# A graph network kernel: the check of its input in pieces behind the first additions of the last pass, and the last edge tile as a group of its own

## The chip, the cores and the metric

The kernel runs on one core of one Trainium2 chip. The metric is the device time of one execution in microseconds (us). In the profile PE is TensorE, DVE is VectorE, ACT is ScalarE, POOL is GpSimd and SP is the engine that queues most DMAs.

## The reference

The graph has 3125 nodes with 128 features and 53125 edges, sorted by `dst`. Three SAGE convolutions are followed by one GINE convolution, each block behind a LayerNorm and a ReLU:

```python
h = jnp.maximum(_layernorm(x, axis=-1), 0.0)
x = x + L0(h)          # 3 x: (segment_sum(h[src], dst) / count) @ Wl.T + b + h @ Wr.T
h = jnp.maximum(_layernorm(x, axis=-1), 0.0)
messages = gelu(h[src] + edge_attr @ We1 ...) @ We2 ...   # _mlp(x[src] + edge_attr, We1, be1, We2, be2)
x = x + mlp(h + segment_sum(messages, dst), Wu1, bu1, Wu2, bu2)
```

## The kernel before

`fast_path` works in two stages, and five instruction streams (one for each engine) meet at semaphores.

**Stage one: the dense stage.** A matrix of edge counts (`f_adj`, one byte for each pair of nodes) is built from the edge list in 213 groups, `GB` in the code. A class `Plan` gives each step a slot; each engine walks the slots in order. From slot 213 on no edges are left, and PE runs the products of the count matrix with the three parts of h (`dense_unit`, L1132). The nodes are cut into 7 chunks c: six of 500 nodes, and chunk 6 with 125. For layer 0 and chunk 6 the chain is `dense_unit` (PE), `mean_rows` (DVE, L664, the sums times the inverse counts), `mix_layer` (PE, L1104 and L1107, which waits for `mean_rows`). On DVE `mean_rows(6)` comes in slot 222, behind `split_rest` (L635) and `split_low` (L640) of slot 221. On PE `mix_layer(6)` comes in slot 223, behind 9 dense units of the next layer's first chunk. A PE instruction that waits holds everything behind it.

**Stage two: the edge pass.** 416 tiles of 128 edges (`FT`) go in groups of 4 (`FTG`): 104 groups g before. Every ninth group up to 98 is "picked" (11 groups): its rows of h are taken from on-chip memory by matmuls with one-hot matrices (`take_sources`, L1183). The other 93 groups get theirs by indirect DMAs, one for each tile, which POOL issues (L545): 372 in a row. POOL writes into a ring of `RW = 6` groups, so the first tile of group number r (counted without the picked ones) waits until group r - 6 has been added. For each group:

- PE: `mix`, edge features times `We1`, two groups ahead (L1168)
- DVE: the one-hots of the destination nodes, two groups ahead (L751), the addition of the gathered rows, `pre` (L870), and one-hots for the picked groups (L771)
- ACT: GELU, `msg` (L997)
- PE: the sum over edges, message times one-hot (L1237)

Behind the last group of a chunk of nodes follow that chunk's node steps, at fixed distances in groups: `TAKE` 1 (ACT copies the sums, L982), `MIX` 2 (PE, L1197 and L1199), `SUM` and `UP` 3 (DVE L783, PE L1205, ACT L985), `DOWN` 4 (PE, L1209), `ADD` 5 (DVE, L787), `STORE` 9. Chunk 5 ends with group 100, chunk 6 with the last group.

**The check.** The fast path holds only for inputs with certain bounds on `dst`. `check_input` on DVE tests them (L802 to L835), PE turns the result into one number (L1218), and `keep_flag` writes it to `spill`. If it is set, a general path computes everything again. All of the check stands ahead of the loop over the groups, and PE waits for it ahead of group 0. The check also reads `order`, whose DMAs are queued behind the broadcast of `rstd`.

Of the kernel before, what the change touches and what calls it, by code (L numbers as in the profile page):

```python
# [17 lines left out]
P = 128  # L18
# [10 lines left out]
class Shapes:  # L29


    def __init__(self, n_nodes, n_edges):
# [20 lines left out]
        self.FG = -(-self.FT // self.FTG)  # L53
        self.SLOPE = P * self.FTG * n_nodes / n_edges
        self.window = [(max(0, int(g * self.SLOPE) - self.MARGIN - 1),
# [3 lines left out]
        self.picked = list(range(self.PERIOD - 1, self.FG - self.FTG, self.PERIOD))  # L59
# [14 lines left out]

    def tiles(self, g):
        return min(self.FTG, self.FT - g * self.FTG)
# [144 lines left out]
def fast_path(nc, s, t, table, counts, inv, outT, spill):  # L221
# [5 lines left out]
    EVEN = NP + NP % 2  # L227
    KEYS = s.A_COLS + s.DW * NB - s.B_FROM
# [9 lines left out]
    END = G + STORE + 1  # L238
    with ExitStack() as ctx:
# [104 lines left out]
        order_in, checked, flagged, be2_ready = sem("order_in"), sem("checked"), sem("flagged"), sem("be2_ready")  # L344

# [57 lines left out]
        def edge_columns(g):  # L403
            return t["edge_attr_T"][:, g * T * P:(g * T + s.tiles(g)) * P]
# [15 lines left out]
        def src_columns(i):  # L420
            g = s.picked[i]
            return t["src_row"][g * T * P:(g + 1) * T * P].partition_broadcast(P)
# [84 lines left out]
        def _(pool):  # L507
# [30 lines left out]
            for g in range(G):  # L538
# [3 lines left out]
                for j in range(s.tiles(g)):  # L542
                    if j == 0 and r >= RW:
# [3 lines left out]
                        in_offset=bass.IndirectOffsetOnAxis(ap=table_idx[:, g * T + j:g * T + j + 1], axis=0),  # L547
# [3 lines left out]
        def _(dve):  # L551
# [149 lines left out]

            dve.wait_ge(idx_in, 16)
            edge_keys(0, HEAD)
            dve.wait_ge(made, 3)
            for slot in range(plan.slots):
# [26 lines left out]
                for c in plan.due("rows_add", slot):  # L732
                    keep_rows(c)

# [11 lines left out]
            def window_onehots(g):  # L746
# [3 lines left out]
                for j in range(s.tiles(g)):  # L750
                    ins = dve.tensor_scalar(onehot[:, g % OH, j, 0:hi - lo], iota[:, 0:hi - lo], float(lo),  # L751
                                            dst_abs[:, g * T + j:g * T + j + 1], ALU.add, ALU.is_equal)
# [37 lines left out]
            def check_input():  # L790

                F, L = first[0:1, :], last[0:1, :]
                F2, L2, FB, LB = F[:, 0:NT:2], L[:, 0:NT:2], F[:, 1:NT:2], L[:, 1:NT:2]
                DG = s.DG
                n_at = [0]

                def more(count):
                    n_at[0] += count
                    return viol[0:1, n_at[0] - count:n_at[0]]

                def over(a, gap, b):
                    dve.scalar_tensor_tensor(out=more(a.shape[-1]), in0=a, scalar=float(gap), in1=b, op0=ALU.subtract,  # L802
                                             op1=ALU.is_gt).then_inc(checked, 1)
                over(L2, s.A_COLS // NB - 1, F2)
                over(F2[:, 0:DG], -float(s.B_FROM // NB), FB)
                over(LB, s.DW - 1, F2[:, 0:DG])
                over(L2[:, 0:DG], -1.0, F2[:, 1:DG + 1])
                over(F2[:, 1:DG + 1], s.DW, F2[:, 0:DG])
                over(F, -1.0, L)
                dve.tensor_scalar(bound[0:1, 0, :], iota[0:1, 0:G], s.SLOPE, -float(s.MARGIN), ALU.mult,  # L810
                                  ALU.add).then_inc(flagged, 1)
# [4 lines left out]
                over(bound[0:1, 0, :], 0.0, group_ends[0:1, 0, :])  # L816
                over(group_ends[0:1, 1, :], 0.0, bound[0:1, 1, :])
                small = [(0, 0.0, ALU.is_gt), (NT - 1, float(N - s.DW), ALU.is_lt)]
                small += [(s.DT * (g + 1), float(e), ALU.is_lt) for e, g in zip(s.node_end, s.build_group) if g + 1 < GB]
                for i, limit, op in small:  # L820
                    dve.tensor_scalar(more(1), F[:, i:i + 1], limit, None, op).then_inc(checked, 1)
                dve.wait_ge(checked, 8 + len(small))
                dve.memset(flag[:, :], 0.0).then_inc(flagged, 1)
                dve.wait_ge(flagged, 3)
                dve.tensor_reduce(flag[0:1, 0:1], viol[0:1, 0:n_at[0]], AX.X, ALU.max).then_inc(flagged, 1)
                dve.wait_ge(order_in, 32)
# [1001 lines left out]
```

## Time and profile before

| what | value |
|---|---|
| median of 3 runs | 976.62 us |
| lowest, highest of the 3 | 975.94, 2135.52 us |
| the profiled execution | 981.04 us |
| its span, first to last instruction | 979.3 us |
| mean granted TensorE clock | 0.965 |
| busy: PE, DVE, ACT, POOL | 879.7, 485.6, 250.2, 383.6 us |

The median and the profiled execution agree within 0.5%; the one run of 2135.52 us stands apart from both. The span leaves out 1.7 us of the profiled execution. The edge pass takes the second half: POOL's first gather starts at 487.91 us, its last at 959.43 us.

### The profile page before, as it was taken

How to read it: one execution, taken by the hardware profiler on the slowest of the kernel's cores; microseconds unless marked ns; L12 is line 12 of the kernel's file. 1: busy time of each engine (PE TensorE's matmuls, PEld its weight loads, DVE VectorE, ACT ScalarE, POOL GpSimd, SP SyncE). 2: the span in 40 equal slices, each digit the busy share in tenths (PEclk: the TensorE clock that was granted, in tenths of full speed). 3: DMA queues.
4: the chain of work that ended last, by engine and by line, in shares of the span. 5: the costliest groups of instructions: out<-in, count | busy, mean ns of one | idle time of the engine just before them, and what ended most of it. 6: DMA issues, size and time to landing. Idle time of an engine off the chain costs nothing.

```text
span 979.3 us, 20510 instructions
## 1 busy us (share of the span) xinstructions
PE 879.7 (90%) x7824; PEld 653.8 (67%) x7824; DVE 485.6 (50%) x1882; ACT 250.2 (26%) x433; POOL 383.6 (39%) x411
## 2 busy tenths in 40 slices
PE   2977999999999999999809999999999899899883
PEld 1733555555554455555609999998988888898882
DVE  6589999995111121121348545445445545445431
ACT  2576677773110110011102111111111111111111
POOL 2000000000000001111277777777777777777771
PEclk9969999999999999999959999999999999999987
DMA  4200001102000000000174444444434444434321
GB/s 137 63 2 12 3 13 13 12 13 65 1 1 1 1 1 11 11 10 17 49 170 108 134 120 137 133 113 130 138 102 134 117 117 130 117 107 130 106 63 32
DMA packets 46635, 67.90 MB, mean 69 GB/s; under 512 B 15396, under 2 KB 25349, under 8 KB 46402
## 3 DMA queue, kind: packets, MB, share of 16 engines
q1 hardware_dynamic: 34626, 42.11, 15.5%
q0 software_dynamic: 11904, 24.40, 9.8%
q8 instruction: 64, 1.05, 0.4%
q14 instruction: 41, 0.34, 0.1%
HBM read 63.18 MB, written 3.30 MB: 68 GB/s over the span
## 4 chain that ended last, share of the span: by engine, by line
PE 64%; DVE 12%; POOL 10%; issue 7%; DMA 3%; ACT 2%; SPq 0%; ACTq 0%; POOLq 0%; DVEq 0%
PE f_ps L1132 26%; PE f_ps L1183 11%; POOL f_adj L545 10%; PE f_ps L1237 8%; PE f_ps L1168 7%; DVE f_region L594 2%; PE f_ps L1017 2%; DVE f_region L592 2%; PE f_ps L1010 2%; PE f_ps L1107 2%; DVE f_region L598 2%; DVE f_region L596 2%; DMA f_adj<-in_dst_next 1%; DMA inv<-f_rstd 1%; PE f_ps L1069 1%
## 5 line engine op out<-in xcount | busy, mean ns | idle before, releaser
L545 POOL DMA_INDIRECT f_adj<-table,f_table_idx x372 | 359.4, 966 | 113.4 <-issue 112.8
L1132 PE MATMUL f_ps<-f_adj,f_parts 125*128 125x500 fp8e4 (+1 forms) x1575 | 331.5, 352 | 0.1
L1132 PEld LDWEIGHTS f_ps<-f_adj,f_parts 125*128 125x128 bf16 x1575 | 143.5, 97 | 130.0 <-issue 11.1
L1183 PE MATMUL f_ps<-f_parts 125*128 125x128 bf16 x3300 | 200.0, 220 | 0.0
L1183 PEld LDWEIGHTS f_ps<-f_parts 125*128 125x128 bf16 x3300 | 193.2, 98 | 6.4 <-issue 4.4
L530 POOL TENSOR_TENSOR f_rest<-f_region,f_parts 125x512 f32<-125x512 f32 (+1 forms) x7 | 7.3, 1050 | 461.5 <-ACT f_parts L975 461.5
L1237 PE MATMUL f_ps<-f_adj 128*128 128x94 f32 (+20 forms) x984 | 131.9, 280 | 30.3 <-ACT f_adj L997 28.2
L870 DVE TENSOR_TENSOR f_adj<-f_ps,f_adj 128x512 f32<-128x512 f32 x93 | 64.1, 689 | 186.1 <-issue 116.0
L1237 PEld LDWEIGHTS f_ps<-f_adj 128*128 128x128 f32 x984 | 120.9, 195 | 37.9 <-issue 34.3
L997 ACT ACTIVATE f_adj<-f_adj 128x512 f32<-128x512 f32 x93 | 58.4, 630 | 336.8 <-DVE f_adj L870 332.5
L887 ACT CAST f_adj<-f_ps 128x500 f32 x213 | 126.1, 592 | 56.7 <-PE f_ps L1017 40.8
L1168 PE MATMUL f_ps<-f_We,f_region 128*128 128x128 f32 x832 | 115.7, 283 | 0.8 <-DVE f_region L696 0.8
L1168 PEld LDWEIGHTS f_ps<-f_We,f_region 128*128 128x128 f32 x832 | 103.5, 196 | 0.9 <-issue 0.9
L751 DVE TENSOR_SCALAR f_adj<-f_iota,f_dst_abs 128x94 f32<-128x94 f16 (+4 forms) x416 | 88.6, 284 | 20.5 <-PE f_ps L1237 20.3
L1010 PE MATMUL f_ps<-f_region 125*128 125x300 f16 (+1 forms) x213 | 65.1, 305 | 30.2 <-DVE f_region L598 28.4
L1017 PE MATMUL f_ps<-f_region 125*128 125x375 f16 x212 | 71.4, 337 | 0.0
L771 DVE TENSOR_SCALAR f_parts<-f_parts 128x512 bf16<-128x512 f16 x275 | 68.6, 304 | 0.4
L592 DVE TENSOR_SCALAR f_region<-f_iota,f_key 125x300 f16<-125x300 f16 x212 | 61.7, 291 | 14.0 <-PE f_ps L1017 13.6
L594 DVE TENSOR_SCALAR f_region<-f_iota,f_key 125x375 f16<-125x375 f16 x212 | 66.6, 314 | 0.0
L1010 PEld LDWEIGHTS f_ps<-f_region 125*128 125x128 f16 x213 | 21.6, 101 | 66.0 <-ACT f_adj L887 26.1
L598 DVE TENSOR_SCALAR f_region<-f_iota,f_low 125x126 f16<-125x126 f16 x213 | 52.7, 247 | 0.0
L596 DVE TENSOR_SCALAR f_region<-f_iota,f_low 125x126 f16<-125x126 f16 x212 | 52.4, 247 | 0.0
(135 smaller groups left out, 478.7 us busy)
## 6 DMA issues: line engine op xcount, KB each, us to landing
f_region<-in_edge_attr_T SPq DMA_DIRECT2D x104, 256.0 KB
f_adj<-table,f_table_idx POOLq DMA_INDIRECT x372
f_parts<-in_src_row SPq DMA_DIRECT2D x11, 256.0 KB, 3.7
f_adj<-inv SPq DMA_DIRECT2D x1, 1562.5 KB, 7.7
table<-f_region SPq DMA_DIRECT2D x6, 250.0 KB
out<-f_xT SPq DMA_DIRECT2D x6, 250.0 KB, 2.5
f_rcntT<-inv SPq DMA_DIRECT2D x5, 250.0 KB, 3.8
f_xT<-in_xT SPq DMA_DIRECT2D x1, 812.5 KB, 6.0
```

The source lines that it names most:

```text
L545: pool.indirect_dma_start(out=rows[:, r % RW, j * D:(j + 1) * D], out_offset=None, in_=table, in_offset=bass.IndirectOffsetOnAxis(ap=table ...
L592: dve.tensor_scalar(keys[0:EP, slot, 0:s.A_COLS], iota[0:EP, 0:s.A_COLS], key[0:EP, tt:tt + 1], None, ALU.is_equal)
L594: dve.tensor_scalar(keys[0:EP, slot, s.A_COLS:KEYS], iota[0:EP, s.B_FROM:s.DW * NB], key[0:EP, tt + 1:tt + 2], None, ALU.is_equal)
L598: dve.tensor_scalar(lows[0:EP, slot, 0, 0:EVEN], iota[0:EP, 0:EVEN], low[0:EP, tt:tt + 1], None, ALU.is_equal).then_inc(onehots, 1)
L751: ins = dve.tensor_scalar(onehot[:, g % OH, j, 0:hi - lo], iota[:, 0:hi - lo], float(lo), dst_abs[:, g * T + j:g * T + j + 1], ALU.add, AL ...
L887: act.copy(adj[:, :, bass.ds(base, s.DW)], ps[:, build_ps(g):build_ps(g) + s.DW * NB].rearrange("p (w b) -> p b w", b=NB)).then_inc(kept, 1)
L1010: pe.matmul(ps[:, o:o + wide], lows[0:EP, slot, 0, :], keys[0:EP, slot, 0:wide], start=True, stop=g == 0, skip_group_check=True)
L1017: ins = pe.matmul(ps[:, o + s.B_FROM:o + s.DW * NB], lows[0:EP, slot, 1, :], keys[0:EP, slot, s.A_COLS:KEYS], start=False, stop=True, skip ...
L1132: ins = pe.matmul(ps[:, dense_ps(i):dense_ps(i) + width(c)], parts[0:NP, (l % 2) * 3 + p, b, :], adj[0:NP, b, lo:hi].bitcast(F8), start=b ...
L1168: ins = pe.matmul(z_ps(g, j), ea[:, g % EA, j * P:(j + 1) * P], weights["We1"][:, :], start=not held, stop=not held, skip_group_check=held)
L1183: ins = pe.matmul(z_ps(g, j), select[0:NP, u % SELECT, j * P:(j + 1) * P], parts[0:NP, 3 + p, b, :], start=b == 0 and j == 0 and p == 0, s ...
L1237: ins = pe.matmul(agg_ps(c, lo, hi), msg[:, g % MS, j * D:(j + 1) * D], onehot[:, g % OH, j, at_lo:at_lo + hi - lo], start=opens and j == ...
```

## The change

1. **The check in pieces.** `check_input` is gone. Its comparisons are run on DVE at the ends of groups 0, 1 and 2, the reductions at the ends of groups 4, 8, 9 and 10. PE makes the number ahead of group 12 in place of group 0, and DVE stores it ahead of group 13 in place of group 2.
2. **The test of the counts** (the maximum over `f_c25`, 25 x 3125 bytes) goes to the dense stage: `check_repeats`, three DVE instructions at the end of slot `CALM = GB + 8 = 221`.
3. **The last tile apart.** `FG` is 105 in place of 104: group 103 has 3 tiles and group 104 has one. Chunk 6 now ends with group 104. The picked groups stay the same.
4. **The padding.** The last tile has 5 edges and 123 padded places. Their source row was row 0 for all; now it is 0 to 122. The host's array `group_ends` follows the new groups.

```diff
+    CALM = GB + 8
+    FLAG, KEEP = 12, 13
+            def check_repeats():
+                dve.memset(flag[:, :], 0.0).then_inc(cleared, 1)
+                dve.wait_ge(cleared, 1)
+                dve.wait_ge(count_in[0], 16 * ((NC + 1) // 2))
+                dve.wait_ge(count_in[1], 16 * (NC // 2))
+                dve.tensor_reduce(flag[0:NB, 2:3], c25[0:NB, :], AX.X, ALU.max).then_inc(repeats, 1)
+                dve.wait_ge(repeats, 1)
+                dve.tensor_scalar(flag[0:NB, 2:3], flag[0:NB, 2:3], 15.5, None, ALU.is_gt).then_inc(repeats, 1)
...
                 for c in plan.due("rows_add", slot):
                     keep_rows(c)
+                if slot == CALM:
+                    check_repeats()
...
-            check_input()
             for g in range(END):
-                if g == 2:
+                if g == KEEP:
                     keep_flag()
...
+                if g == 0:
+                    check_tiles()
+                if g == 1:
+                    check_steps()
+                if g == 2:
+                    check_windows()
+                if g == 4:
+                    join_checks()
+                if g == 8:
+                    check_order()
+                if g == 9:
+                    join_order()
+                if g == 10:
+                    join_all()
...
-                if g == 0:
-                    pe.wait_ge(flagged, 9)
+                if g == FLAG:
+                    pe.wait_ge(flagged, 6)
...
-        self.FG = -(-self.FT // self.FTG)
+        self.FG = -(-(self.FT - 1) // self.FTG) + 1
...
-    a["src_tiles"] = np.pad(src, (0, pad)).reshape(-1, P).T
+    a["src_tiles"] = np.concatenate([src, np.arange(pad, dtype=src.dtype)]).reshape(-1, P).T
```

DVE around slot 221 of the dense stage, before. The third row is `mean_rows(6)`, 125 columns wide:

```order
L635 TENSOR_TENSOR f_rest<-f_ps,f_parts 125x512 [waits f_lowest,f_mid,f_high]
L640 TENSOR_TENSOR f_parts<-f_rest,f_parts 125x512 [waits f_mid]
L664 TENSOR_TENSOR f_work<-f_ps,f_rcntT 128x125 [waits f_mixed,f_rcnt_ready,f_dense_done]
L635 TENSOR_TENSOR f_rest<-f_ps,f_parts 125x128 [waits f_lowest,f_mid,f_high]
```

The same place on DVE after the change:

```order
L642 TENSOR_TENSOR f_rest<-f_ps,f_parts 125x512 [waits f_lowest,f_mid,f_high]
L647 TENSOR_TENSOR f_parts<-f_rest,f_parts 125x512 [waits f_mid]
L710 MEMSET f_flag 128x4
L714 TENSOR_REDUCE f_flag<-f_c 25x1 [waits f_count_in1,f_count_in0,f_cleared]
L716 TENSOR_SCALAR f_flag<-f_flag 25x1 [waits f_repeats]
L671 TENSOR_TENSOR f_work<-f_ps,f_rcntT 128x125 [waits f_mixed,f_rcnt_ready,f_dense_done]
L642 TENSOR_TENSOR f_rest<-f_ps,f_parts 125x128 [waits f_lowest,f_mid,f_high]
```

Three instructions now stand between `split_low` and `mean_rows(6)`.

DVE at the head of the edge pass, before, from the middle of the check to the first addition (L870):

```order
L821 TENSOR_SCALAR f_adj<-f_first 1x1 x8
L823 MEMSET f_flag 128x4 [waits f_checked]
L825 TENSOR_REDUCE f_flag<-f_adj 1x1 [waits f_flagged]
L827 TENSOR_TENSOR f_adj<-f_adj 125x425 [waits f_order_in]
L830 TENSOR_REDUCE f_flag<-f_adj 125x1 [waits f_flagged]
L831 TENSOR_REDUCE f_flag<-f_c 25x1
L833 TENSOR_SCALAR f_flag<-f_flag 25x1 [waits f_flagged]
L835 TENSOR_REDUCE f_flag<-f_flag 128x1 [waits f_flagged]
L751 TENSOR_SCALAR f_adj<-f_iota,f_dst_abs 128x94 x4
L870 TENSOR_TENSOR f_adj<-f_ps,f_adj 128x512 [waits f_gathered0,f_z_ready]
```

The same place after, where L897 is the addition:

```order
L789 TENSOR_SCALAR f_parts<-f_parts 128x512 x2
L769 TENSOR_SCALAR f_adj<-f_iota,f_dst_abs 128x94 x4
L897 TENSOR_TENSOR f_adj<-f_ps,f_adj 128x512 [waits f_gathered0,f_z_ready]
L789 TENSOR_SCALAR f_parts<-f_parts 128x512 x3
L818 SCALAR_TENSOR_TENSOR f_adj<-f_last,f_first 1x213
L818 SCALAR_TENSOR_TENSOR f_adj<-f_first 1x212
L818 SCALAR_TENSOR_TENSOR f_adj<-f_last,f_first 1x212
```

The first addition no longer stands behind the check, nor behind the wait for `order`.

PE at the end of the edge pass, before:

```order
L1205 MATMUL f_ps<-f_rcntT,f_Wu 128x500 [waits f_node_summed]
L1237 MATMUL f_ps<-f_adj 128x54 [waits f_msg_ready,f_oh_ready]
L1237 MATMUL f_ps<-f_adj 128x54 x3
L1209 MATMUL f_ps<-f_hT,f_Wu 128x500 [waits f_up_active]
L1197 MATMUL f_ps<-f_adj,f_We 128x125 [waits f_pre_ready,f_taken]
```

The same place after:

```order
L1246 MATMUL f_ps<-f_rcntT,f_Wu 128x500 [waits f_node_summed]
L1278 MATMUL f_ps<-f_adj 128x54 [waits f_msg_ready,f_oh_ready]
L1278 MATMUL f_ps<-f_adj 128x54 x2
L1250 MATMUL f_ps<-f_hT,f_Wu 128x500 [waits f_up_active]
L1278 MATMUL f_ps<-f_adj 128x32 [waits f_msg_ready,f_oh_ready]
L1238 MATMUL f_ps<-f_adj,f_We 128x125 [waits f_pre_ready,f_taken]
```

The `DOWN` step of chunk 5 stood behind all sums over edges; it now stands between those of group 103 and that of group 104.

## Rows read from the trace of the kernel before

**Rows 1.** Page, part 4: the chain that ended last, by engine

```profile
PE 64%; DVE 12%; POOL 10%; issue 7%; DMA 3%; ACT 2%; SPq 0%; ACTq 0%; POOLq 0%; DVEq 0%
```

**Rows 2.** POOL's gathers: the page's group, then the view of line 545

```profile
L545 POOL DMA_INDIRECT f_adj<-table,f_table_idx x372 | 359.4, 966 | 113.4 <-issue 112.8
...
L545 POOL DMA_INDIRECT f_adj<-table,f_table_idx x372: 940/945/1599, 487.9 to 959.4; - x186
```

**Rows 3.** Timeline (start us, us, engine, line), head of the edge pass

```profile
487.91 1.14 POOL L545 DMA_INDIRECT f_adj<-table,f_table_idx  x1 [0.40 <-issue]
...
494.44 1.15 POOL L545 DMA_INDIRECT f_adj<-table,f_table_idx  x1 [0.30 <-issue]
...
511.08 0.60 DVE L827 TENSOR_TENSOR f_adj<-f_adj 125x425 f32<-125x425 int32 x1 [12.34 <-DMA f_adj<-in_dst_next]
...
512.23 3.38 DVE L831 TENSOR_REDUCE f_flag<-f_c 25x1 f32<-25x3125 uint8 x1
...
516.61 0.68 DVE L870 TENSOR_TENSOR f_adj<-f_ps,f_adj 128x512 f32<-128x512 f32 x1
...
518.36 0.95 POOL L545 DMA_INDIRECT f_adj<-table,f_table_idx  x1 [0.30 <-issue]
```

**Rows 4.** Chain in order of time (start us, us, what), 240 to 275 us

```profile
250.35 3.86 PE f_ps L1132 x22
254.22 0.22 PE f_ps L1104 x2
```

**Rows 5.** Timeline, DVE in the dense stage: `mean_rows(6)`

```profile
252.99 0.28 DVE L664 TENSOR_TENSOR f_work<-f_ps,f_rcntT 128x125 f32<-128x125 f32 x1
```

**Rows 6.** Timeline, DVE in the check: the two short instructions beside L831

```profile
496.73 0.06 DVE L823 MEMSET f_flag<- 128x4 f32 x1
...
515.65 0.14 DVE L833 TENSOR_SCALAR f_flag<-f_flag 25x1 f32<-25x1 f32 x1
```

**Rows 7.** Timeline, end of the edge pass

```profile
949.45 0.94 POOL L545 DMA_INDIRECT f_adj<-table,f_table_idx  x1 [0.30 <-issue]
...
952.01 0.69 DVE L870 TENSOR_TENSOR f_adj<-f_ps,f_adj 128x512 f32<-128x512 f32 x1 [3.69 <-issue]
...
958.18 0.95 POOL L545 DMA_INDIRECT f_adj<-table,f_table_idx  x1 [0.30 <-issue]
...
959.43 0.94 POOL L545 DMA_INDIRECT f_adj<-table,f_table_idx  x1 [0.30 <-issue]
...
960.85 0.68 ACT L985 ACTIVATE f_hT<-f_ps,f_bu 128x500 f32<-128x500 f32 x1 [2.15 <-PE f_ps L1205]
963.01 0.69 DVE L870 TENSOR_TENSOR f_adj<-f_ps,f_adj 128x512 f32<-128x512 f32 x1 [4.39 <-issue]
963.74 0.63 ACT L997 ACTIVATE f_adj<-f_adj 128x512 f32<-128x512 f32 x1 [2.21 <-DVE f_adj L870]
...
966.47 0.27 ACT L982 COPY f_adj<-f_ps 128x125 f32<-128x125 f32 x1 [2.11 <-PE f_ps L1237]
...
969.00 0.29 DVE L783 TENSOR_TENSOR f_rcntT<-f_rcntT,f_ps 128x125 f32<-128x125 f32 x1
```

**Rows 8.** Chain in order of time, end of the edge pass

```profile
964.51 1.93 PE f_ps L1237 x8
966.43 1.79 PE f_ps L1209 x2
```

**Rows 9.** Stretches: us, busy (x instructions) by engine, granted clock, DMA share, GB/s

```profile
481.30:484.70 3.40, 0.93 (x7) 0.55 (x5) 1.68 (x8) 1.23 (x5) 1.44 (x2) 1.00 0.13 32
484.70:488.10 3.40, 3.29 (x15) 3.32 (x16) 2.82 (x6) 1.58 (x2) 2.77 (x6) 0.50 0.63 168
...
948.90:955.80 6.90, 6.90 (x31) 6.58 (x31) 0.69 (x1) 1.21 (x2) 5.07 (x7) 0.51 0.19 49
```

**Rows 10.** Timeline, PE: idle stretches (in brackets)

```profile
948.50 1.77 PE L1237 MATMUL f_ps<-f_adj 128*128 128x20 f32 x9 [1.98 <-ACT f_adj L997]
...
710.83 1.10 PE L1237 MATMUL f_ps<-f_adj 128*128 128x94 f32 x8 [1.63 <-ACT f_adj L997]
```

More of the change, by code:

```diff
@@ L73, in cols, with tile @@
         return c * self.NBC * self.NP, self.node_end[c]
+    def tile(self, g):
+        return min(g * self.FTG, self.FT - 1) if g < self.FG else self.FT
     def tiles(self, g):
-        return min(self.FTG, self.FT - g * self.FTG)
+        return self.tile(g + 1) - self.tile(g)
     def by_rows(self, g):
@@ L403, in edge_columns @@
         def edge_columns(g):
-            return t["edge_attr_T"][:, g * T * P:(g * T + s.tiles(g)) * P]
+            return t["edge_attr_T"][:, s.tile(g) * P:s.tile(g + 1) * P]
         def agg_ps(c, lo, hi):
@@ L751, in window_onehots @@
                     ins = dve.tensor_scalar(onehot[:, g % OH, j, 0:hi - lo], iota[:, 0:hi - lo], float(lo),
-                                            dst_abs[:, g * T + j:g * T + j + 1], ALU.add, ALU.is_equal)
+                                            dst_abs[:, s.tile(g) + j:s.tile(g) + j + 1], ALU.add, ALU.is_equal)
                 ins.then_inc(oh_ready, 1)
@@ L788, in node_add, with more, over, check_tiles @@
                                          op0=ALU.add, op1=ALU.add).then_inc(node_added, 1)
[L790 to L803, printed above, removed]
+            F, L = first[0:1, :], last[0:1, :]
+            F2, L2, FB, LB = F[:, 0:NT:2], L[:, 0:NT:2], F[:, 1:NT:2], L[:, 1:NT:2]
+            DG = s.DG
+            n_at = [0]
+            def more(count):
+                n_at[0] += count
+                return viol[0:1, n_at[0] - count:n_at[0]]
+            def over(a, gap, b):
+                dve.scalar_tensor_tensor(out=more(a.shape[-1]), in0=a, scalar=float(gap), in1=b, op0=ALU.subtract,
+                                         op1=ALU.is_gt).then_inc(checked, 1)
+            small = [(0, 0.0, ALU.is_gt), (NT - 1, float(N - s.DW), ALU.is_lt)]
+            small += [(s.DT * (g + 1), float(e), ALU.is_lt) for e, g in zip(s.node_end, s.build_group) if g + 1 < GB]
+            def check_tiles():
                 over(L2, s.A_COLS // NB - 1, F2)
@@ L866, in _ @@
                         dve.wait_ge(z_ready, g + 1)
-                        dve.wait_ge(gathered[r % RW], 16 * (T * (r // RW) + s.tiles(g)))
+                        dve.wait_ge(gathered[r % RW], 16 * sum(s.tiles(s.of_ordinal(q)) for q in range(r % RW, r + 1, RW)))
                         if r >= PR:
```

45 lines of the change are left out of this document (24 added, 21 removed).

## The prediction

> **What bounds the kernel now.** The page's chain comes first. It puts 64% of the span on PE and only 10% on POOL [rows 1], and taken alone it says that the edge pass is PE's. The view of POOL's own line says otherwise. Its 372 gathers take 0.966 us each in the mean, and the idle time ahead of them is issue time alone, 112.8 us, or 0.305 us each [rows 2]. So POOL goes from one gather to the next: 372 x (0.966 + 0.305) = 473 us, and from the first start at 487.91 to the end of the last at 959.43 + 0.94 = 960.37 it is 472.5 us. No addition and no buffer ever held it. PE and DVE only have to keep up, and the chain runs along PE while PE works off the backlog of its late start. The end of the kernel is therefore three things in a row: when POOL may start, 472.5 us of gathers, and what follows the last gather.
>
> The start is set by the dense stage, where PE is the path: in the chain in order of time the dense products are followed by `mix_layer(6)` with nothing between [rows 4].
>
> **Part 1, the first addition moves ahead of the check.** Before, DVE waits 12.34 us for `order` inside the check and then runs the reductions; the first addition starts at 516.61 us and ends at 517.29 [rows 3]. After, it needs only the first group's four gathers: they end about 492.8 us (487.91 plus 4 x 1.25, less the gap), and with 1.6 to 2.0 us to land (below) and DVE's one-hots ahead of it that is about 495 us. This gains 21 us for DVE and PE, and nothing at the end, unless POOL was held. POOL may run 6 groups, 24 gathers, ahead. The 25th, counted along the timeline, starts at 518.36 us [rows 3], 1.07 us after the addition that it needs. The cover is thin, but it is there, and the value of the move is 0 beyond it. POOL's gathers are slower than 0.94 us now and then. Through DVE's catching up this may change by a little: the excess over 0.94 us is 372 x 0.026 = 9.7 us in all, about 0.6 us in 30 us; I take 0.5 us as gained from a calmer head of the pass, with bounds of 1.5 us gained and 1.5 us lost.
>
> The pieces of the check then lie beside the gathers, in DVE time that DVE has: a group lasts 4 gathers, 5.1 us, and DVE is busy for half of the whole span. The longest piece is under 2 us. POOL asks for an addition only six groups later. Cost 0; if that cover were gone, it would be about the 6 us that the pieces last together. PE's wait for the flag goes from group 0 to group 12, where the flag is done since group 10: 0.
>
> **Part 2, the test of the counts in the dense stage.** This is the term that I expect to decide the sign. In slot 221 it stands between `split_low` and `mean_rows(6)` on DVE. Before, `mean_rows(6)` starts at 252.99 us with no idle time ahead of it [rows 5]: its input was ready, and DVE comes late already. Ahead of it come now the memset, 0.06 us, and 0.04 to the next [rows 6], the reduction, 3.38 us [rows 3], 0.04 for the wait, and the comparison, 0.14 us [rows 6]. That is 3.6 to 3.7 us, and `mean_rows(6)` starts at 256.6 and ends at 256.9 us. PE's `mix_layer(6)` waits for it; before it starts in the chain at 254.22 us, right behind the dense products [rows 4], so the slack was 254.22 - 253.27 = 0.95 us. After, it starts about 257.0 us. **PE stands still for 2.8 us**, and behind it in PE's queue are all dense units of the two layers left. PE is busy without a gap before and after, so nothing takes this up again: POOL's first gather is 2.8 us later. The bounds are 2.5 us (the short instructions overlap) and 3.1 us (the weight load ahead of the product is no longer hidden). At the old place the reduction cost nothing, since POOL covered it. So 3.4 us of DVE time that were free are moved to where nothing covers them.
>
> The clock comes on top. In the stretch 481.3 to 484.7 us PE is busy 0.93 us of 3.4, and in the next 3.4 us the granted clock is 0.50, which is the level of 1.2 GHz [rows 9]. At 948.50 PE had stood still 1.98 us, and the clock is 0.51 for the 6.9 us from 948.9 on, though PE is busy all of them [rows 9, 10]. After 1.63 us of idle time at 710.83 it stayed at 1.00 [rows 10]. Our idle stretch of 2.8 us is longer than the one that was followed by the fall, so I expect it to fall. A dense product at half clock takes twice its time: 3.4 us at half clock lose 1.7 us, 6.9 us lose 3.45. I take 1.7, because the load behind the stall is full; the bounds are 0 and 3.45.
>
> **Part 3, the end of the pass.** Before: last gather ends 960.37, addition 963.01, GELU 963.74, sums 964.51 + 1.93, then chunk 5's `DOWN` of 1.79 us, which delays chunk 6's `MIX` to 968.22, although ACT has copied the sums by 966.74 [rows 7, 8]. After, with all times on the old scale:
>
> - Group 103 has 3 tiles; its last gather is the one at 958.18, which ends 959.13 us. The usual distance to the addition is 952.01 - (949.45 + 0.94) = 1.62 us [rows 7]. So it starts at 960.75. The width goes from 512 to 384: between 0.69 us for 512 and 0.29 us for 125 columns [rows 7] that is 0.56 us, end 961.3.
> - ACT is in chunk 5's GELU until 961.53 [rows 7]. Then group 103's follows, 0.5 us, by 962.05, and PE starts its sums at about 962.2 in place of 964.51 us.
> - Six records in place of eight: 1.93 x 6/8 = 1.45 us, to 963.65. `DOWN`: 1.79, to 965.45.
> - Group 104's single tile was gathered by 960.37. Even at the 2.64 us that the last gather needed before (963.01 - 960.37, with its 123 equal rows) its message is there at 963.7 us. So **the new padding gains nothing at the end**; `DOWN` covers it by 1.7 us. Its sums are two records, 0.5 us, to 965.95.
> - ACT's copy, 0.27 us [rows 7], no longer lies beside `DOWN`: with the handovers and the weight load 0.5 us, to 966.45. Chunk 6's `MIX` starts there in place of 968.22: **1.8 us gained**. The rest is as before.
>
> The clock is low in this stretch before. At full clock the sums and `DOWN` would take 1.6 us less, which is 3.4 us gained; with the low clock in chunk 6's steps instead about 1 us is lost, so 0.8 us gained. These are the bounds.
>
> **The sum.** +2.8 (stall) + 1.7 (clock) - 1.8 (end) - 0.5 (head) = +2.2 us. The profiled execution had 981.04 us, 979.3 of span and 1.7 around it, which the change leaves alone; it would be 983.2. The median of the runs is 4.4 us under the profiled one; the terms are the same there, so 976.62 + 2.2 = 978.8 us.
>
> **Rivals.**
>
> - *The stall without a fall of the clock*: +0.5 us, 977.1. For it speaks that PE is full right up to the gap and right behind it. Chance 0.24.
> - *The clock low for 6.9 us*: +3.9 us, 980.5, as after 948.9. Chance 0.13.
> - *The head was on the path after all (faster)*. The page's chain has PE in it for 64%. If PE's start set the end, the 21 us would come through: 978.8 - 21 = 958 us, some 1.9% faster. It decides where POOL stands: only if gathers wait for additions can an earlier addition move the end. The rows say that they do not, by 1.07 us at the nearest point, and without the profiler the margin may be a little less, for a gain of a microsecond. Chance 0.04.
> - *The test of the counts costs nothing (faster)*. If PE reached `mix_layer(6)` later than in this trace by the 2.8 us, only the end and the head would be left: -2.3 us, 974.3. Against it stands a queue in fixed order. Chance 0.07.
> - *POOL's gathers get slower (slower)*. The gather at 494.44 us, beside the comparisons of the check, took 1.15 us in place of 0.94 [rows 3]. DVE's work is now spread over gathers that ran beside a waiting DVE. If that doubled the excess of all 372 gathers, it would add 9.7 us: 988.5 us. It decides against us from a mean of about 1.02 us on. Against it: the same instructions lay beside gathers before, and the catching up disappears. Chance 0.04.
>
> [...]
>
> **How the numbers follow.** The forecast has 0.45, the five rivals 0.24, 0.13, 0.04, 0.07 and 0.04, and 0.03 is for what I do not see. The likeliest is 978.8 us. The range takes the forecast with its bounds and the first two clock rivals: from 977.1 less the 1.6 us of a better end and about 1 us of a better head, 974.5, to 980.5 with an end worse by 1.0, 981.7 with the rest. That is about 0.8. A change of 2% is 19.5 us, which is about what a measurement of this kernel can tell from none. No case but those of 0.04 comes near it: faster by over 2% 0.01, slower 0.01, same 0.98.
>
> **What the new profile would show.** A gap of 2.5 to 3.1 us on PE ahead of L1104's successor at about 254.3 us, ended by `mean_rows`, and a granted clock of 0.5 just behind it. POOL's first gather at about 492.4 us, 372 gathers without a wait, and the first addition about 498 us. At the end PE's chunk 5 `DOWN` between two groups of sums, and from the end of the last gather to the start of chunk 6's `MIX` 6.1 us in place of 7.85. I am wrong if PE has no gap there, if POOL's row names DVE as a releaser with more than 1 us, or if the mean gather moves by more than 5 ns.

## The result, and the profile after

The changed kernel takes 981.03 us in the median of 7 runs (979.51 to 986.25), the kernel before 976.91 us in the runs beside it (its one run of 2135.52 us stands apart and is left out). The ratio is 1.005, interval 1.0031 to 1.0069: 4.1 us slower by the medians, 4.9 us by the ratio. That is far within 2%, inside the range of 974.5 to 981.7, and twice the +2.2 us of the forecast. The profiled execution took 979.51 us with a span of 977.5 us. It is shorter than the profiled execution of before, 981.04 us, which happened to lie 4.4 us over its kernel's median. So the times say what the change costs, and the two traces say where.

**The stall in the dense stage** is there. The first view is the timeline of DVE and PE (start us, us, engine, line, in brackets the idle time before it and what ended it):

```profile
248.58 0.69 DVE L647 TENSOR_TENSOR f_parts<-f_rest,f_parts 125x512 bf16<-125x512 f32 x1 [0.68 <-ACT f_parts L974]
249.23 0.06 DVE L710 MEMSET f_flag<- 128x4 f32 x1
249.33 3.40 DVE L714 TENSOR_REDUCE f_flag<-f_c 25x1 f32<-25x3125 uint8 x1
252.76 0.14 DVE L716 TENSOR_SCALAR f_flag<-f_flag 25x1 f32<-25x1 f32 x1
252.87 0.29 DVE L671 TENSOR_TENSOR f_work<-f_ps,f_rcntT 128x125 f32<-128x125 f32 x1
...
253.31 0.46 PE L1145 MATMUL f_ps<-f_work,f_W1l 128*128 128x125 f32 x2 [2.89 <-DVE f_work L671]
```

The three new instructions fill 249.23 to 252.90 us on DVE, and `mean_rows(6)`, which started in its turn before [rows 5], comes right behind them. PE has stood still for 2.89 us; before it had gone from the dense products to `mix_layer(6)` with nothing between [rows 4]. In this one trace the clock stays at full speed behind the gap, 1.00 from 252.9 to 259.7 us.

**POOL** still goes from one gather to the next, and the chain says so now, as [rows 1] did not. First its line of engines on the page, then the group of the gathers, then the view of line 552:

```profile
POOL 37%; PE 36%; issue 12%; DVE 11%; DMA 2%; ACT 1%; ACTq 0%; POOLq 0%; SPq 0%; DVEq 0%
...
L552 POOL DMA_INDIRECT f_adj<-table,f_table_idx x372 | 359.9, 967 | 113.7 <-issue 112.8
...
L552 POOL DMA_INDIRECT f_adj<-table,f_table_idx x372: 940/944/2422, 487.4 to 959.5; - x186
```

PE had 64% of the chain before. The additions now begin at 498.00 us in place of 516.61, PE has no backlog to work off, and the chain runs along POOL instead. The kernel got no shorter by it: the issue time is 112.8 us in both, and the mean gather 967 ns against 966 [rows 2]. But the longest of 372 gathers was 1599 ns before and is 2422 ns now. Here it is, in the timeline of POOL and DVE at the head of the edge pass:

```profile
517.13 0.97 POOL L552 DMA_INDIRECT f_adj<-table,f_table_idx  x1 [0.30 <-issue]
517.41 1.91 DVE L849 TENSOR_REDUCE f_flag<-f_adj 1x1 f32<-1x1704 f32 x1
518.40 2.42 POOL L552 DMA_INDIRECT f_adj<-table,f_table_idx  x1 [0.30 <-issue]
519.25 0.72 DVE L795 SCALAR_TENSOR_TENSOR f_rcntT<-f_hT,f_eps,f_adj 128x500 f32<-128x500 f32 x1
519.89 0.96 DVE L769 TENSOR_SCALAR f_adj<-f_iota,f_dst_abs 128x94 f32<-128x94 f16 x4
...
521.13 0.94 POOL L552 DMA_INDIRECT f_adj<-table,f_table_idx  x1 [0.31 <-issue]
```

L849 is the reduction of `join_checks`, a piece of the check in group 4. Behind it, with no wait between, come `node_scale` (L795, both inputs in SBUF) and the one-hots. The gather that started beside the reduction ends at 518.40 + 2.42 = 520.82 us, and the one-hots at 519.89 + 0.96 = 520.85. The next gather takes 0.94 us again, though another `node_scale` starts beside it (at 521.81 us).

**The end of the pass**, in the chain in order of time (start us, us, what):

```profile
958.23 3.62 DMA f_adj<-table,f_table_idx
...
961.94 0.57 DVE f_adj L897
...
962.53 0.53 ACT f_adj L1038
...
963.20 0.84 PE f_ps L1278 x6
964.04 0.90 PE f_ps L1250 x2
964.94 0.28 PE f_ps L1278 x2
...
965.56 0.79 PE f_ps L1238 x2
...
969.12 0.35 DVE f_xT L805
```

`DOWN` (L1250) stands between the sums of group 103 and the two records of group 104, and group 104's message is there when `DOWN` ends: the order that the prediction drew. The times are different. The last gather starts at 959.48 and ends at 960.42 us, so chunk 6's `MIX` (L1238) follows it by 5.14 us, against 7.85 before and 6.1 forecast. Group 103's rows took 961.94 - (958.23 + 0.94) = 2.77 us to land in place of 1.62; the sums and `DOWN` ran at full clock, 0.84 and 0.90 us, where [rows 8] has 1.93 for eight records and 1.79 us; and chunk 6's own steps were the slow ones (`MIX` 0.79 us for two records). From the end of the last gather to the end of the last DVE addition of node rows (L805, 969.12 + 0.35) it is 9.05 us, against 10.81 before.

### The profile page after: what moved, and what is told of

The parts are those of the page before. It is cut to its first block, busy times and chain, and to the rows that moved or that the text cites. A ratio compares the mean times of both kernels' runs of the same rounds, so it can differ in the third digit from the quotient of the medians.

```text
span 977.5 us, 20520 instructions
## 1 busy us (share of the span) xinstructions
PE 883.1 (90%) x7824; PEld 655.1 (67%) x7824; DVE 484.8 (50%) x1883; ACT 250.2 (26%) x434; POOL 384.0 (39%) x411
## 4 chain that ended last, share of the span: by engine, by line
POOL 37%; PE 36%; issue 12%; DVE 11%; DMA 2%; ACT 1%; ACTq 0%; POOLq 0%; SPq 0%; DVEq 0%
POOL f_adj L552 37%; PE f_ps L1173 25%; DVE f_region L601 2%; DVE f_region L599 2%; DVE f_region L605 2%; DVE f_region L603 2%; PE f_ps L1058 2%; PE f_ps L1148 2%; PE f_ps L1051 2%; PE f_ps L1110 1%; DMA f_rcntT<-in_dst_pt 1%; ACT f_adj L928 1%; DVE f_parts L627 1%; PE f_ps L1159 1%; PE f_ps L1145 1%
## 5 line engine op out<-in xcount | busy, mean ns | idle before, releaser
L552 POOL DMA_INDIRECT f_adj<-table,f_table_idx x372 | 359.9, 967 | 113.7 <-issue 112.8
L1224 PE MATMUL f_ps<-f_parts 125*128 125x128 bf16 x3300 | 201.6, 221 | 4.2 <-DVE f_parts L789 4.2
L1224 PEld LDWEIGHTS f_ps<-f_parts 125*128 125x128 bf16 x3300 | 194.5, 99 | 10.8 <-issue 8.5
L897 DVE TENSOR_TENSOR f_adj<-f_ps,f_adj 128x512 f32<-128x512 f32 (+1 forms) x94 | 64.3, 685 | 233.5 <-issue 151.0
L1278 PE MATMUL f_ps<-f_adj 128*128 128x94 f32 (+20 forms) x984 | 132.1, 280 | 44.9 <-ACT f_adj L1038 42.2
L1278 PEld LDWEIGHTS f_ps<-f_adj 128*128 128x128 f32 x984 | 120.6, 195 | 56.0 <-issue 52.0
L1038 ACT ACTIVATE f_adj<-f_adj 128x512 f32<-128x512 f32 (+1 forms) x94 | 58.7, 626 | 359.4 <-DVE f_adj L897 355.5
L1209 PE MATMUL f_ps<-f_We,f_region 128*128 128x128 f32 x832 | 116.5, 284 | 0.8 <-DVE f_region L703 0.8
L1209 PEld LDWEIGHTS f_ps<-f_We,f_region 128*128 128x128 f32 x832 | 104.0, 197 | 1.1 <-issue 0.9
```

Of the source, the lines that this page charges most:

```text
L552: pool.indirect_dma_start(out=rows[:, r % RW, j * D:(j + 1) * D], out_offset=None, in_=table, in_offset=bass.IndirectOffsetOnAxis(ap=table ...
L1209: ins = pe.matmul(z_ps(g, j), ea[:, g % EA, j * P:(j + 1) * P], weights["We1"][:, :], start=not held, stop=not held, skip_group_check=held)
L1224: ins = pe.matmul(z_ps(g, j), select[0:NP, u % SELECT, j * P:(j + 1) * P], parts[0:NP, 3 + p, b, :], start=b == 0 and j == 0 and p == 0, s ...
L1278: ins = pe.matmul(agg_ps(c, lo, hi), msg[:, g % MS, j * D:(j + 1) * D], onehot[:, g % OH, j, at_lo:at_lo + hi - lo], start=opens and j == ...
```

## The experiments

Sixteen runs, in sessions that each have their own runs of the kernel before beside them; all ratios are to those. The ratio and the difference of the medians can say different amounts, so both are given where it matters. POOL's stretch is from the start of its first gather to the end of its last; it was 472.5 us before and 473.0 after.

**e1: the test of the counts in slot 221 alone.** Before, and of the change only this:

```diff
+                if slot == CALM:
+                    check_repeats()
```

> The kernel before with one part of the change: the test of the counts (memset, reduction, comparison on DVE) stands in slot 221 of the dense stage; all other comparisons stay ahead of the first group, and the last group keeps its 4 tiles. Theory A (a stall on PE and nothing else): PE stands still 2.9 us ahead of mix_layer(6), the clock stays, and the time is 2.9 us above the kernel before, 979.8. Theory B (the clock falls behind the stall in many runs): 1.7 to 3.5 us more, 981.5 to 983.3 in the median. Theory C (what was lost lies elsewhere, in the pieces or behind the span): under 2 us above the kernel before.

982.27 us against 977.32, ratio 1.0044 (1.0029 to 1.006). The gap on PE is 2.9 us. This one edit costs 4.3 us by the ratio and 5.0 by the medians, as much as the whole change within the intervals.

**e2: the changed kernel without the stall.** Slot 226 is a place where DVE has time:

```diff
-    CALM = GB + 8
+    CALM = GB + 13
```

> The changed kernel with CALM = GB + 13: the same three instructions stand in slot 226, where DVE idled 9 us in the trace of before. Theories A and B: PE has no gap, and the time falls by the whole price of the stall: A to 978.1 less (2.9 us under the changed kernel), B by 4.6 to 6.4 us, to 975 to 976.4, which is under the kernel before. Theory C: no change against the changed kernel, 980 to 981.

976.79 us against 977.32, ratio 0.9999 (0.9985 to 1.0013), and no gap on PE. The stall is a cost, then. But the gain of the end of the pass doesn't show either, and it should have. In the trace two gathers are long (timeline of POOL and DVE):

```profile
514.86 1.91 DVE L849 TENSOR_REDUCE f_flag<-f_adj 1x1 f32<-1x1704 f32 x1
515.66 2.62 POOL L552 DMA_INDIRECT f_adj<-table,f_table_idx  x1 [0.30 <-issue]
516.70 0.72 DVE L795 SCALAR_TENSOR_TENSOR f_rcntT<-f_hT,f_eps,f_adj 128x500 f32<-128x500 f32 x1
517.34 0.96 DVE L769 TENSOR_SCALAR f_adj<-f_iota,f_dst_abs 128x94 f32<-128x94 f16 x4
518.06 0.67 DVE L897 TENSOR_TENSOR f_adj<-f_ps,f_adj 128x512 f32<-128x512 f32 x1
518.59 2.24 POOL L552 DMA_INDIRECT f_adj<-table,f_table_idx  x1 [0.30 <-issue]
519.26 0.72 DVE L795 SCALAR_TENSOR_TENSOR f_rcntT<-f_hT,f_eps,f_adj 128x500 f32<-128x500 f32 x1
519.91 0.94 DVE L769 TENSOR_SCALAR f_adj<-f_iota,f_dst_abs 128x95 f32<-128x95 f16 x4
```

Again the first ends with the one-hots: 518.28 and 518.30 us. The second has no reduction beside it. It starts in the next row of DVE instructions and ends with its one-hots (518.59 + 2.24 = 520.83; they end at 520.85). e3 and e9 have such a second long gather too, of 2.24 and 2.22 us; in the changed kernel's own trace the gather at 521.13, beside the same instructions, took 0.94. Why one is long and the other isn't stays open.

**e3: the pieces alone.** The check in pieces, the test of the counts a piece too (end of group 3), the old groups and padding:

```diff
+                if g == 3:
+                    check_repeats()
```

> The kernel before with the check in pieces behind the first additions; the test of the counts is one more piece at the end of group 3, nothing is put into the dense stage, the last group keeps its 4 tiles and the old padding. Theories A and B: POOL is not held before, so the earlier start of DVE and PE is worth 0 to 0.5 us: 976.4 to 977. Theory C: the pieces cost 2 to 4 us through slower gathers, 979 to 981.

980.05 us against 977.32, ratio 1.0031 (1.002 to 1.0043): 2.7 us slower by the medians, 3.0 by the ratio. The prediction had this edit at nothing. The longest gather is 2.87 us, and POOL's stretch 475.2 us, the longest outside e9 to e11:

```profile
516.99 1.91 DVE L847 TENSOR_REDUCE f_flag<-f_adj 1x1 f32<-1x1702 f32 x1
517.54 2.87 POOL L552 DMA_INDIRECT f_adj<-table,f_table_idx  x1 [0.31 <-issue]
518.82 0.72 DVE L793 SCALAR_TENSOR_TENSOR f_rcntT<-f_hT,f_eps,f_adj 128x500 f32<-128x500 f32 x1
519.47 0.97 DVE L767 TENSOR_SCALAR f_adj<-f_iota,f_dst_abs 128x94 f32<-128x94 f16 x4
```

**e4: the last tile and the padding alone**, the whole check in front of the pass as before:

```diff
-        self.FG = -(-self.FT // self.FTG)
+        self.FG = -(-(self.FT - 1) // self.FTG) + 1
```

> The kernel before with the last tile as a group of its own and the padding to rows 0 to 122; the whole check stays ahead of the first group. Theories A and B: 1.7 to 1.8 us under the kernel before, 975.2. Theory C: the 1.7 us seen in one trace are given back behind the last store, and the time is that of the kernel before or above.

975.32 us against 977.32, ratio 0.9993 (0.9976 to 1.0011): not to be told from before by the ratio (0.7 us faster, with an interval from 2.3 faster to 1.1 slower), 2.0 us faster by the medians. No gather takes over 1.4 us. Its chain of the end shows what the gain can be when nothing lands late and the clock is full:

```profile
957.53 0.57 DVE f_adj L906
...
958.79 0.84 PE f_ps L1273 x6
959.64 0.90 PE f_ps L1245 x2
960.54 0.15 PE f_ps L1273 x2
...
961.03 0.49 PE f_ps L1233 x2
```

The last gather ended at 957.18 us (956.24 + 0.94), `MIX` follows it by 3.85 us, and the end of the last node rows by 6.7 us in place of 10.81.

**e5 and e6: two ways to part the reduction from `node_scale`,** both from e2. e5 moves the joining pieces behind the last `node_scale`, e6 moves the seven `node_scale` steps and leaves the pieces:

```diff
-                if g == 4:
+                if g == 10:
                     join_checks()
-                if g == 8:
+                if g == 11:
                     check_order()
-                if g == 9:
+                if g == 12:
                     join_order()
-                if g == 10:
+                if g == 13:
                     join_all()
...
-    FLAG, KEEP = 12, 13
+    FLAG, KEEP = 15, 16
```

```diff
-                if 3 <= g < 3 + NC:
-                    node_scale(g - 3)
+                if 11 <= g < 11 + NC:
+                    node_scale(g - 11)
```

> The kernel of e2 (the whole change, the test of the counts in slot 226) with the reduction over the comparisons (L849) moved from group 4 to group 10, the later pieces to groups 11 to 13, the flag to groups 15 and 16. Groups 3 to 9 hold a scaling of node columns (node_scale, two inputs in SBUF) right behind the pieces. Theory D: the gathers of 2.2 to 2.9 us near 515 to 521 us in the traces of the kernels with pieces come from the reduction with node_scale and the one-hots queued behind it without a wait; then no gather is over 1.6 us, POOL's stretch from first to last gather is 471.5 us in place of 472.8, and the time is 1 to 2 us under e2, about 975. Theory E (the early additions and the edge loads that they release make the traffic at that time): the long gathers stay at 515 to 521 us and the time is that of e2.

> The kernel of e2 with node_scale in groups 11 to 17 in place of 3 to 9; the pieces of the check stay where the change put them. Theory D: the reduction of group 4 has one-hots with a wait behind it, and no gather near 520 us is over 1.6 us; gathers beside the scalings at 545 to 580 us may be lengthened by 0.1 to 0.3 us each. The time is 1 to 2 us under e2. Theory E: as e2, with the long gathers at 515 to 521 us.

e5: 974.85 us against 977.99, ratio 0.9964 (0.9952 to 0.9977). e6: 975.1 us, ratio 0.9966 (0.9953 to 0.9978). Both beat the kernel before, and both get there. The views of line 552 of e2, e5 and e6, in this order (duration of a gather min/median/max):

```profile
L552 POOL DMA_INDIRECT f_adj<-table,f_table_idx x372: 940/944/2624, 484.8 to 957.6; - x186
```

```profile
L552 POOL DMA_INDIRECT f_adj<-table,f_table_idx x372: 940/944/1274, 485.1 to 955.2; - x186
```

```profile
L552 POOL DMA_INDIRECT f_adj<-table,f_table_idx x372: 940/944/1394, 485.6 to 956.3; - x186
```

In e6 the reduction is where it was, and the gathers beside it are short:

```profile
516.22 1.91 DVE L849 TENSOR_REDUCE f_flag<-f_adj 1x1 f32<-1x1704 f32 x1
516.82 0.94 POOL L552 DMA_INDIRECT f_adj<-table,f_table_idx  x1 [0.30 <-issue]
518.05 0.98 DVE L769 TENSOR_SCALAR f_adj<-f_iota,f_dst_abs 128x94 f32<-128x94 f16 x4
518.07 0.94 POOL L552 DMA_INDIRECT f_adj<-table,f_table_idx  x1 [0.31 <-issue]
```

So neither the reduction alone (e6) nor `node_scale` alone (e5) makes the gathers over 2 us; they come where the second is queued right behind the first. None of the eight traces with the joining pieces late (e5 and e10 to e16) has a gather over 1.71 us, and all four with both in place (the changed kernel, e2, e3, e9) have one of 2.42 to 2.87.

**e7: the padding alone,** in the kernel before; **e8: the kernel before again,** as a control:

```diff
-    a["src_tiles"] = np.pad(src, (0, pad)).reshape(-1, P).T
+    a["src_tiles"] = np.concatenate([src, np.arange(pad, dtype=src.dtype)]).reshape(-1, P).T
```

> The kernel before with one line changed: the 123 padded places of the last tile name rows 0 to 122 in place of row 0. In the traces of the kernels with the old padding the addition follows the end of the last gather by 2.62 to 2.64 us, against 1.6 for other groups. If equal rows are the reason, it is 1.6 to 1.7 us here and the kernel is 1.0 us faster, 976.3; if the last gather is slow for another reason, both stay as they are.

> The kernel before against itself. It shows what two profiles and two sets of runs of one kernel differ by: the ratio is 1 within 0.2%, and POOL's first gather starts anywhere between 483.7 and 488 us, as in the traces of kernels whose dense stage is that of before; POOL's stretch is 471.5 to 472.0 us, and no gather is over 1.6 us.

e7: 975.26 us against 977.99, ratio 0.9969 (0.9948 to 0.999). e8: 977.57 us, ratio 0.9999 (0.9989 to 1.0008). The timelines of e7 and then of e8, the last gather and the addition behind it:

```profile
961.43 0.94 POOL L545 DMA_INDIRECT f_adj<-table,f_table_idx  x1 [0.30 <-issue]
963.98 0.69 DVE L870 TENSOR_TENSOR f_adj<-f_ps,f_adj 128x512 f32<-128x512 f32 x1 [2.74 <-DMA f_adj<-table,f_table_idx]
```

```profile
954.97 0.94 POOL L545 DMA_INDIRECT f_adj<-table,f_table_idx  x1 [0.30 <-issue]
958.52 0.69 DVE L870 TENSOR_TENSOR f_adj<-f_ps,f_adj 128x512 f32<-128x512 f32 x1 [4.49 <-DMA f_adj<-table,f_table_idx]
```

From the end of the gather to the addition it is 1.61 us in e7 and 2.61 us in e8; with the old padding it was 2.64, 2.63 and 2.62 us in the traces of before, e1 and e3 as well. The 123 equal source rows cost 1.0 us in landing: the last tile with different rows has 1.55 to 1.68 us in eight more traces (e2, e4 to e6, e12, e14 to e16), and with equal rows 2.76 in e13. The interval of e7 reaches from 1 to 5 us gained, and the trace accounts for 1.

**e9 to e11** were to part the changed kernel into its terms, in one session.

> The changed kernel as it is, once more, beside the next two in one call. By the terms found so far (stall 2.9 to 4.3, gathers behind the reduction 1.3 to 2.7, end of the pass 3 to 4 us gained) it comes to 0.5 to 4 us above the kernel before; the first measurement said 4.9, interval 3.0 to 6.7. One gather of over 2 us is expected again at 515 to 521 us.

> The changed kernel with the pieces of e5 (reduction in group 10 and so on) but with the test of the counts left in slot 221: e5 with the stall. If the stall costs what its gap lasts, it is 2.9 us above e5 (0.9964 of before), a ratio of 0.9994; if the clock falls behind the stall in many executions, 4.5 to 6.4 us above e5, a ratio of 1.001 to 1.003. No gather over 1.6 us. Against e9 it shows what the long gathers cost in the changed kernel: 1.3 to 2.7 us.

> The kernel of e5 with the old padding (row 0 for all 123 padded places). Theory F (step of the prediction): DOWN of chunk 5 covers the later landing, nothing changes against e5, ratio 0.9964, although the last addition comes 1.0 us later. Theory G: PE runs the end at full clock, DOWN is over by then, and up to 1.0 us is lost, ratio 0.9974.

Beside these three the kernel before takes 1189.87 us. The changed kernel took 1199.69 us, ratio 1.0085 (1.0055 to 1.0114); with the joining pieces late 1195.78, ratio 1.004 (1.0011 to 1.0068); that with slot 226 and the old padding 1192.07, ratio 1.0003 (0.9977 to 1.0029). The view of what POOL waited for in e9 (us, times) has a wait that the other sessions lack, and the view of PE's waits (us, times, longest us) shows what lies behind it:

```profile
  DVE f_adj L897: 200.4, 47
  issue: 101.7, 324
```

```profile
PE f_ps L1224 <- issue: 120.6, 153, 2.5
```

The additions come late, and the ring of six groups holds POOL for 200 us; in e10 it is 206.1 us, in e11 211.0. But the additions don't wait for their rows: in e9 DVE waited 9.1 us for gathers ahead of them, in the first trace of the changed kernel 12.1. It is PE that stops. In the middle of runs of equal matmuls it stands still with nothing in the profile to wait for, 120.6 us at L1224 and 157.8 with L1278 and L1209, and the first trace has no such stop at L1224. From 505 to 955 us its granted clock is 0.79, against 0.99 there, and DVE's one-hots, which reuse buffers that PE frees, wait 310 us. Why PE stops is open, and so is what the chip has to do with it: the record gives these three and e5 to e8 the same chip number. The three ratios come in the same order as in the other sessions, and the gap of 2.9 us and the long gathers (2.62 and 2.22 us in e9) are there too, but the sizes can't be carried over.

**e12 and e13** are e10 and e11 again, in a session where the kernel before takes 977.38 us. e12 is the changed kernel with e5's late pieces and the stall in slot 221; e13 is e5 with the old padding. The expectation of e12 puts the wait of POOL down to gathers that land late, which the traces don't bear out.

> The kernel of e10 again, since e9 to e11 fell on a chip on which the gathers land so late that POOL is held by its ring for 200 us, and the end of POOL's row is no longer the bound of before. If the stall costs what its gap lasts, the ratio to the kernel before is 0.9994 (e5's 0.9964 and 2.9 us); if the clock falls behind the stall in many executions, 1.001 to 1.003. Against the changed kernel's 1.005 it gives the price of the long gathers there: 1.3 to 2.7 us are expected.

> The kernel of e11 again, for the same reason: e5 with the old padding. Theory F (DOWN of chunk 5 covers the later landing): ratio 0.9964 as e5. Theory G (at full clock DOWN is over before): 0.9974. In the trace the last addition starts 2.6 us after the end of the last gather, and PE either waits for the last message or does not.

e12: 979.73 us against 977.38, ratio 1.0021 (1.0007 to 1.0035). e13: 976.81 us, ratio 0.9989 (0.9974 to 1.0005). Against e5 and its repetition e14 the old padding costs 1.1 us by the plain mean of the times, with an interval from -0.4 to 2.5 us, and 1.6 us when each is set against the kernel before measured beside it: not settled. In its trace PE did not wait for group 104's message.

**e14 to e16** give the stall its price: e14 is e5 again, e15 is e12 again, and e16 has the reduction over the counts twice:

```diff
                 dve.tensor_reduce(flag[0:NB, 2:3], c25[0:NB, :], AX.X, ALU.max).then_inc(repeats, 1)
                 dve.wait_ge(repeats, 1)
+                dve.tensor_reduce(flag[0:NB, 2:3], c25[0:NB, :], AX.X, ALU.max).then_inc(repeats, 1)
+                dve.wait_ge(repeats, 2)
```

> The kernel of e5 again, as the partner of the next two on one chip: the test of the counts in slot 226, no stall. Ratio to the kernel before 0.9964 within 0.0015.

> The kernel of e12 again: the same with the test in slot 221. Of the five traces of kernels with this stall one (e12) shows the clock at half for 3.4 us behind the gap. If that is the rule of all executions, the price of the stall in the mean is 2.9 us plus a fifth of 1.7, 3.2 us above e14. If the clock falls more often than the traces say, 4 to 6 us.

> The kernel of e15 with the reduction over the counts made twice in slot 221 (the second changes nothing in the result). The gap on PE grows from 2.9 to 6.3 us. Without any effect of the clock it costs 3.4 us more than e15. With a gap of 6.3 us the clock should be seen to fall in the trace, behind or in the gap, and then it costs 3.4 us and 0 to 3.4 us more; that shows what a fall behind the stall is worth.

e14: 974.8 us against 977.84, ratio 0.9981 (0.9964 to 0.9999). e15: 979.4, ratio 1.0019 (1.0006 to 1.0032). e16: 985.06, ratio 1.008 (1.0062 to 1.0099). With the runs of equal kernels put together (e12 and e15, 24 runs; e5 and e14, 22 runs), and plain times compared, one stall costs 4.2 us in the mean (3.1 to 5.3), and the double one 5.1 us more than the single (3.2 to 6.7). In e12 and in e15 the clock fell, from 0.5 us before the end of the gap on. The timeline of PE in e15, and the stretch behind it (us, busy and instructions of PE, weight loads, DVE, ACT, POOL, then the granted clock):

```profile
254.40 0.76 PE L1145 MATMUL f_ps<-f_work,f_W1l 128*128 128x125 f32 x2 [2.89 <-DVE f_work L671]
...
255.38 3.04 PE L1173 MATMUL f_ps<-f_adj,f_parts 125*128 125x500 fp8e4 x9
...
258.48 3.75 PE L1173 MATMUL f_ps<-f_adj,f_parts 125*128 125x500 fp8e4 x17
...
253.90:257.30 3.40, 2.90 (x9) 1.70 (x10) 0.35 (x2) 0.37 (x1) 0.00 (x0) 0.51 0.01 2
```

And the same two views of e16:

```profile
256.76 0.76 PE L1147 MATMUL f_ps<-f_work,f_W1l 128*128 128x125 f32 x2 [6.32 <-DVE f_work L671]
...
255.30:262.10 6.80, 5.34 (x16) 3.00 (x17) 1.28 (x3) 0.37 (x1) 0.00 (x0) 0.50 0.00 1
```

From the start of L1145 to the second run of dense products it is 2.64 us in the trace of the changed kernel at full clock (253.31 to 255.95), and 4.08 us in e15 with 3.4 us at 0.51: a loss of 1.44 us. In e12 the same distance is 4.07 us. The low stretch of e16 starts 1.5 us before its gap ends.

## Why the prediction was off by half

**The step that failed** is in part 1, "the pieces of the check then lie beside the gathers ... Cost 0", with its half microsecond gained from a calmer head and its bounds of 1.5 us to both sides. The pieces cost 3.0 us alone by the ratio of e3. Their place beside `node_scale` costs 1.9 us in e2 against e5 and e14 (0.7 to 3.1), and 2.7 us in the changed kernel against e12 and e15 (1.0 to 4.7). I had asked only whether DVE has time for them, and it has. What counts is what they do to a POOL that never rests: while POOL sets the end, each microsecond by which a gather gets longer is one of the kernel. The rival "POOL's gathers get slower" had the right place and the wrong shape. Not all 372 got slower by a little, but one or two by 1.3 to 1.9 us each (in the changed kernel's trace one, by 1.5 us, so the rest of its 2.7 us has no source there; the interval allows that there is no rest), and the mean that I wanted to watch (5 ns) moves by 1 ns.

The Trainium skill, "SBUF — State Buffer", section "Who interferes with whom", says that on this chip a reduction never contends with GpSimd. It also says that a VectorE instruction with two inputs in SBUF contends with a GpSimd instruction that reads SBUF, and not with one that only writes it. The traces agree on the reduction where no instruction with two inputs in SBUF is right behind it (0.94 us, e6). What they show with `node_scale` behind it follows from neither sentence: a gather that starts under the reduction ends only with the one-hots behind both, 2.42, 2.62 and 2.87 us in three traces, though `node_scale` itself lasts 0.72 us. That parting the pair takes the long gathers away is shown from both sides, by e5 and by e6. That a lock of a port, asked for by the second instruction and kept through the row, is what holds the gather would be a guess from the ends that coincide; no run shows it, and the second long gathers of e2, e3 and e9, which have no reduction beside them, need a further reason.

**The stall** was right: 2.89 or 2.90 us of gap in each of the six traces that have the test in slot 221 once, against 2.8 forecast with bounds of 2.5 and 3.1.

**The clock behind it** was right in kind and too sure. It fell in two traces of six, for 3.4 us and 1.44 us lost where it did (1.7 forecast). One in three would make 2.9 + 0.5 = 3.4 us, which the times allow: they say 4.2 (3.1 to 5.3), against 4.5 forecast for both. With 6.3 us of idle time (e16) the clock was half for 6.8 us.

**The end of the pass** was right as a sum, by luck in its parts. The trace of the changed kernel gains 10.81 - 9.05 = 1.8 us, the forecast to the digit. But up to the start of `MIX`, for which the forecast was made, it gains 7.85 - 5.14 = 2.7 us, with a later landing (2.77 us for 1.62) and a full clock in the sums and `DOWN`. Behind it, with a half clock in chunk 6's steps, it loses 0.9. In eight other traces with the tile apart the distance is 6.7 to 7.9 us, which is 2.9 to 4.1 us gained and about what I had put as the bound of a full clock, 3.4 us; it is 8.7 in e13. The distance of the old grouping varies as well, from 10.4 to 11.4 us in five traces. The times of e5 and e14 agree: about 3 us faster than before. But e4, which has the end and the padding and nothing else of the change, gains 0.7 us by its ratio and 2.0 by its medians, and why e5 gains more is open.

**The padding** was said to gain nothing at the end. As the last tile stands apart this is what e13's trace shows: group 104's message is there before `DOWN` ends. The 8.7 us of that trace go with group 103's rows, which landed 2.47 us after their last gather; they did so in 2.46 us in e14, with the new padding. The times don't settle it. By itself it is worth the 1.0 us by which equal rows land later, which I had not foreseen.

**The sum** with the measured terms: stall and clock +4.2, the place of the pieces +2.7, end and padding with the rest of the change -2.7 (the mean of the medians of e5 and e14 against those beside them is -3.1, of the ratios -2.7): +4.2 us. Measured were +4.1 by the medians and +4.9 by the ratio. This is no check of the terms, since each is the difference of two kernels in one row, from before to e5, to e12, to the changed kernel, and such differences add up by themselves. The edits made alone are the check: e1 +4.3, e3 +3.0 and e4 -0.7 us by the ratios make +6.6, by the medians +5.7, which is more than the whole but not beyond the three intervals together. No run has the early first addition by itself. That it gained nothing, as forecast, fits the waits: POOL's waits for additions are 0.6 us in two places in the trace of before, and the same in e5.

**The span of a single profile** says nothing of terms this small. It fell by 1.8 us while the times rose by 4. The start of POOL's first gather lies between 483.7 and 490.5 us in the ten traces that have no gap on PE (483.68 in e3, 490.5 in e7), though nothing in the dense stage of those two differs from before. From `mix_layer(6)` to that start it is 233.9 to 234.2 us in all ten, so what varies lies ahead of it, and it is larger than any term of the sum. Within one kernel POOL's stretch varies too: 471.1 us in e5 and 473.0 in e14. Only e3's 475.2 stands clear of that.

**A version that beats the kernel before** is e5: 974.85 and 974.8 us in two sessions against 977.99 and 977.84, ratios 0.9964 (0.9952 to 0.9977) and 0.9981 (0.9964 to 0.9999), where the changed kernel has 1.005 (1.0031 to 1.0069). It keeps all of the change but moves the test of the counts to slot 226 and the joining pieces behind the last `node_scale`.

## What to carry to other kernels

Work that is moved off a place where an idle engine covers it must be priced at its new place by who waits behind it there: 3.6 us of DVE time that cost nothing beside POOL's gathers cost 4.2 us as a stall of PE, and nothing that showed five slots later. When one engine issues gathers without a rest and sets the end, look at what each moved instruction of another engine does to single gathers, by their longest and not by their mean. A term of a few microseconds is read from many runs or from a distance within a trace, never from the spans of two profiles.

## What the runs showed of the hardware

- A gather of POOL that starts beside a DVE reduction of 1.91 us, with an instruction of two SBUF inputs queued right behind it, took 2.42 to 2.87 us in place of 0.94, and ended within 0.03 us of DVE's row of instructions (the changed kernel, e2, e3). Beside the same reduction with one-hots behind it: 0.94 us (e6).
- An indirect gather of 128 rows of which 123 are the same row let the addition start 2.61 to 2.76 us after its end; with different rows 1.55 to 1.68 us.
- With 2.89 us of idle PE the granted clock fell to 0.51 for 3.4 us in two traces of six (e12, e15); with 6.32 us it was 0.50 for 6.8 us in the one trace (e16).
- The changed kernel took 981 us in one session and 1200 us in another (e9), where PE stopped for 158 us within its runs of matmuls, with nothing in the profile to wait for, and POOL waited 200 us for additions. The reason is open.
